# Expert weights split during the attention, routing by lists written batch by batch, and expert outputs added into x2 in memory, in one program

## What is computed

```python
x = x + tanh(g_xattn[0]) * xattn(ctx, layernorm(x), ...)   # keys and values from the context and from x itself
xf = layernorm(x)
gate_scores = softmax(xf @ gate_w)                         # 8 experts
topk_scores, topk_idx = top_k(gate_scores, 2); topk_scores /= sum(topk_scores)
h = gelu(xf @ w1[e] + b1[e]);  y = h @ w2[e] + b2[e]       # w1: 256 x 1024, w2: 1024 x 256 for each expert e
out = x + tanh(g_ffn[0]) * (topk_scores[0] * y[topk_idx[0]] + topk_scores[1] * y[topk_idx[1]])
```

## Time and profile before

| what | value |
|---|---|
| time, median of 3 runs | 1904.99 us (1902.63 to 1905.17) |
| the profiled execution's own time | 1902.62 us |
| its span in the trace | 1900.9 us |
| busy share of the span | PE 88%, PEld 61%, DVE 75%, ACT 63%, POOL 62% |
| mean granted clock of PE | 0.951 of 2.4 GHz |

### The profile page before, as it was taken

The page is one execution under the profiler, slowest core; times in us unless marked ns, Lnnn a source line. Parts: engine busy times, 40 slices in busy tenths (PEclk is TensorE's granted clock), DMA queues, the critical chain, the costliest instruction groups (busy, mean ns, idle before and its releaser), DMA issues. The chain is left out here.

```text
span 1900.9 us, 42714 instructions
## 1 busy us (share of the span) xinstructions
PE 1674.2 (88%) x15031; PEld 1163.1 (61%) x15032; DVE 1428.0 (75%) x2917; ACT 1195.3 (63%) x2666; POOL 1183.0 (62%) x1297
## 2 busy tenths in 40 slices
PE   2899999999999999999999999998402999999980
PEld 1456666666666666666666666665302999989970
DVE  4777888888888888888888888877395666666646
ACT  2587777777777777877777777777254333433320
POOL 4477777777777777777777777767263343333320
PEclk9999999999999999999999999999555999999995
DMA  3267766767767666676776776767455111111119
GB/s 131 46 127 140 142 144 131 139 139 142 147 129 145 138 140 144 135 139 138 139 150 136 136 137 129 138 130 142 118 186 173 46 49 45 50 50 47 47 35 289
DMA packets 599541, 233.18 MB, mean 123 GB/s; under 512 B 534064, under 2 KB 584016, under 8 KB 598992
## 3 DMA queue, kind: packets, MB, share of 16 engines
q1 hardware_dynamic: 592656, 212.67, 52.5%
q0 software_dynamic: 6720, 18.36, 3.1%
HBM read 78.66 MB, written 20.19 MB: 52 GB/s over the span
## 5 line engine op out<-in xcount | busy, mean ns | idle before, releaser
L279 POOL TENSOR_TENSOR p_parts<-p_f,p_parts 112x487 f16<-112x487 f32 x512 | 560.4, 1118 | 194.2 <-ACT p_parts L374 194.2
L365 ACT ACTIVATE p_f<-scores_ps,shift 112x487 f32<-112x487 f32 x512 | 337.0, 663 | 13.3 <-DVE shift L500 9.7
L495 DVE TENSOR_REDUCE neg_max<-scores_ps 112x1 f32<-112x487 f32 x512 | 313.0, 654 | 27.1 <-PE scores_ps L653 27.1
L402 ACT ACTIVATE k_hi<-proj_ps 128x488 fp32r<-128x488 f32 x256 | 147.9, 578 | 262.5 <-PE proj_ps L635 262.5
L1018 ACT ACTIVATE space<-h_ps,b_sb,undo 128x256 f32<-128x256 f32 x280 | 142.8, 560 | 232.1 <-PE h_ps L1247 228.8
L374 ACT ACTIVATE p_parts<-p_f 112x487 f16<-112x487 f32 x512 | 275.9, 607 | 0.0
L536 DVE SCALAR_TENSOR_TENSOR v_sb<-proj_ps,v_sb 128x512 f16<-128x512 f32 (+1 forms) x256 | 176.5, 689 | 92.1 <-ACT v_sb L416 89.4
L530 DVE TENSOR_TENSOR k_lo<-proj_ps,k_hi 128x488 fp32r<-128x488 f32 x256 | 168.2, 657 | 78.2 <-ACT k_hi L402 78.0
L684 PE MATMUL pv_ps<-v_sb,pt_sb 128*128 128x128 f16 x2048 | 218.9, 221 | 7.8 <-DMA pt_sb<-p_parts 7.8
L635 PE MATMUL proj_ps<-kv_hi,wkv_hi 128*128 128x488 f16 x512 | 192.3, 376 | 22.0 <-POOL kv_lo L306 13.5
L635 PE MATMUL proj_ps<-wkv_hi,kv_hi 128*128 128x512 f16 (+1 forms) x512 | 194.6, 380 | 0.1
(11 more groups left out here) (222 smaller groups left out, 4075.1 us busy)
## 6 DMA issues: line engine op xcount, KB each, us to landing
w_part<-in_L_ffn_w_dram SPq DMA_DIRECT2D x64, 256.0 KB, 3.5
stage<-in_L_ffn_w_dram SPq DMA_DIRECT2D x32, 512.0 KB, 4.1
ctx_sb<-in_ctx_dram SPq DMA_DIRECT2D x32, 375.0 KB
space<-y_rows SPq DMA_DIRECT2D x32, 224.0 KB, 4.7
pt_sb<-p_parts SPq DMA_TRANSPOSE x256, 4.0
x_sb<-in_x_dram SPq DMA_DIRECT2D x32, 112.0 KB
res_sb<-in_x_dram SPq DMA_DIRECT2D x32, 112.0 KB, 5.3
x_dram<-x_sb SPq DMA_DIRECT2D x32, 112.0 KB, 2.9
```

The lines of the kernel that those rows point to most:

```text
L279: pool.tensor_tensor(p_parts[0:LQ, p % PS, h, 1, 0:LK], p_f[0:LQ, p % 2, h, 0:LK], p_parts[0:LQ, p % PS, h, 0, 0:LK], ALU.subtract).then_i ...
L365: act.activation(p_f[0:LQ, p % 2, h, 0:LK], scores_ps[n][0:LQ, 0:LK], ACT.Exp, bias=shift[0:LQ, p // 2 % 2, n:n + 1], accum_out=row_sum[0: ...
L402: act.activation(k_hi[:, j], ps[:, 0:LKP], ACT.Copy).then_inc(kq_high, 1)
L495: dve.tensor_reduce(neg_max[0:LQ, p // 2 % 2, n:n + 1], scores_ps[n][0:LQ, 0:LK], AX.X, ALU.max, negate=True).then_inc(max_done, 1)
```

## The change

The two blocks become one. The parts are these:

- The large buffers lie in one `arena` with a 16 KB region for each expert. Peaks of w1 and w2 are taken in 32 parts in the steps of batches -1 to 14. From batch 16 on, 32 parts are loaded again, split by ACT and DVE (two operations of 128x512 each), and stored by SP to `split_dram` as float16. SP loads the finished halves into the regions: experts 0 and 1 in the last batch's steps (t = 248 to 255), 2 and 3 at t = 256, 4 to 7 after the last batch's layer norm.
- q and k are split in float16; the scale of the scores moves into the exponential. The maximum is taken over two heads in one instruction, the shift for two pairs in one.
- For each batch, DVE, PE and POOL work out the tokens' places (`onehot`, `prefix`, `rank`) and POOL writes token number and weight into `table_dram` by two indirect DMAs. The last two batches' stages stand in consecutive steps (`EARLY`). At the end one gather reads the lists, and three transposes turn them.
- ACT multiplies each tile of y by its weights, and POOL adds it by indirect DMA into `sums_dram`, which holds x2. The output is four DMAs from there, memory to memory. The expert loop is written out instead of a loop with a counter.

```diff
-        q_hi = sb("q_hi", [128, NP, LQ], F32R)
-        k_hi = sb("k_hi", [128, NP, LKP], F32R)
+        k_hi = region(4, 0, [NP, LKP], F16)
+        q_hi = region(5, 0, [NP, LQ], F16)
...
+STAGES = ("o_turn", "out", "x2", "rstd2", "xn", "xnt", "xnt_copy", "logits", "logits_copy", "top", "ratio", "onehot", "prefix", "rank", "entry")
+USUAL = dict(zip(STAGES, (13, 21, 22, 23, 24, 25, 26, 26, 27, 30, 31, 32, 34, 35, 36)))
+EARLY = {NB - 2: dict(zip(STAGES, range(13, 28))), NB - 1: dict(zip(STAGES, range(13, 28)))}
...
+            def maximum(p):
+                n = 2 * (p % 2)
+                dve.wait_ge(scores_done, 2 * p + 2)
+                dve.tensor_reduce(neg_max[0:LQ, p // 2 % 2, n:n + 2], scores_ps[0:LQ, n:n + 2, 0:LK], AX.X, ALU.max, negate=True).then_inc(max_done, 1)
...
+                if t in SPLIT_STEPS:
+                    part = SPLIT_STEPS.index(t)
+                    for w in range(2):
+                        dve.wait_ge(part_high, 2 * part + w + 1)
+                        dve.scalar_tensor_tensor(out=w_parts[:, w, 1], in0=w_part[:, w], scalar=scale[:, 4 + w:5 + w], in1=w_parts[:, w, 0],
+                                                 op0=ALU.mult, op1=ALU.subtract).then_inc(part_low, 1)
...
+                for ob in batches_at("prefix", t):
+                    pe.wait_ge(hot_done, 2 * ob + 2)
+                    nc.tensor.matmul(tail_ps(ob)[0:LQ, 264:272], before_me[0:LQ, 0:LQ], member[0:LQ, ob % 2], start=True, stop=True)
+                    nc.tensor.matmul(tail_ps(ob)[0:LQ, 272:280], ones[0:LQ, 0:LQ], member[0:LQ, ob % 2], start=True, stop=True).then_inc(prefix_done, 1)
```

The expert loop of POOL, the weighing on ACT (its loop index t handles gelu of tile t + 1), and the output:

```diff
-            for t in range(TILES + 2):
+            for t in range(TILES):
                 if t + 2 < TILES:
                     pool.wait_ge(xt_done, t + 1)
                     gather(t + 2)
-                if t >= 2:
-                    pool.wait_ge(y_ready, t - 1)
-                    for a in range(2):
-                        n = 2 * (t - 2) + a
-                        pool.indirect_dma_start(y_rows, bass.IndirectOffsetOnAxis(ap=y_row_i[:, n:n + 1], axis=0), y_sb[:, t % 2, a], None).then_inc(y_stored[t % 2], 16)
+                pool.wait_ge(y_weighed, t + 1)
+                if t >= 1:
+                    pool.wait_ge(summed[(t - 1) % 2], ((t - 1) // 2 + 1) * 32)
+                for a in range(2):
+                    n = 2 * t + a
+                    pool.indirect_dma_start(sums, bass.IndirectOffsetOnAxis(ap=sums_row[:, n:n + 1], axis=0), yw_sb[:, t % 2, a], None, compute_op=ALU.add).then_inc(summed[t % 2], 16)
...
+                    if m == 1 and t >= 1:
+                        act.wait_ge(y_ready, t)
+                        if t >= 3:
+                            act.wait_ge(summed[(t - 1) % 2], (t - 1) // 2 * 32)
+                        for a in range(2):
+                            n = 2 * (t - 1) + a
+                            last = act.activation(yw_sb[:, (t - 1) % 2, a], y_sb[:, (t - 1) % 2, a], ACT.Copy, scale=weight[:, n:n + 1])
+                        last.then_inc(y_weighed, 1)
...
+            for s in range(2):
+                sp.wait_ge(summed[s], (TILES + 1 - s) // 2 * 32)
+            per = TOKENS // 4
+            for n in range(4):
+                sp.dma_start(out.rearrange("b p d -> (b p) d")[n * per:(n + 1) * per].rearrange("(q r) d -> q (r d)", q=128),
+                             sums[n * per:(n + 1) * per].rearrange("(q r) d -> q (r d)", q=128)).then_inc(out_stored, 16)
```

1158 lines of the change are left out of this document (543 added, 615 removed).

## The result

The changed kernel takes 2486.28 us, median of 4 runs (2485.36 to 2492.66), against 1904.08 (1902.63 to 1905.17) for the kernel before on the same chip: a ratio of 1.3065, 95% interval 1.3041 to 1.309. It is slower, as forecast, but by 582 us instead of 175, and outside the range. The profiled execution's span is 2484.3 us, its mean granted clock 0.897.

The account below looks back on a forecast made before the run. PE was taken to bound the attention and the expert loop. From 1902.6 us, -28 (attention), -65 (to the first tile), -32 (end) and +300 (expert loop) made 2078, predicted as 2080; range for 8 in 10: 2010 to 2160.

Parts of the forecast that it names:

- The attention: Attention batches: float16 score blocks save PE time, gate matmuls add 16 us, DVE stays off the bound; net -28 us.
- the cover: Attention: DMA transposes of probabilities, issued two steps behind the pair, used after four, hide added weight traffic; otherwise 1 us a batch.
- Score blocks: Attention on PE: float16 matmuls save 0.35 us a block of scores, at most 45 us in all.
- The expert loop: PE waits 6.4 us a turn for a gather behind POOL's adds, clock falls: turn 20.3 us, +300 us.
- the clock's price: Expert loop: after each stall PE works at half speed for a while, costing 3.0 us a turn.
- a turn of 22.6 us: Expert loop: adds land in twice 2.46 us and the gather behind waits; time 2155 us.
- adding in memory is slow: Rival, expert loop: slow adds hold up the gather behind them; turn about 22.6 us, time 2155 us; chance 0.13.
- From the attention to the first tile: Stretch from the last attention work to the first h: first h comes earlier, -65 us, from -79 to -45.
- the 14 us charged for the loads: Before the first h: expert weight loads delay the last transpose and small routing transfers, 14 us, between 0 and 30.
- The end: From the last y to the end: 21.7 us instead of 53.9, -32 us; -19 if memory to memory runs at half rate.
- attention stretches: Rival, attention: DMA queues or DVE take the reserve, 1 us or more a batch; 2110 to 2150 us; chance 0.08.
- the likeliest case: As forecast: expert loop turn near 20 us, time 2035 to 2130 us; chance 0.60.

Follow-up runs that it names:

- port repairs: The changed kernel with the maxima of scores and the ranking's place, picked and rank kept in PSUM, order of work as changed: 2384.91 us.
- order repairs: The changed kernel with ranking, peaks and splits moved to the end of VectorE's even steps, all else as changed: 2355.77 us.
- e15_before_f16_psum: The kernel before with only the float16 parts of q and k and what goes with them, and the maxima in PSUM: 1872.76 us, ratio 0.9846.
- e3_gather_ahead: The changed kernel with the expert loop's gathers one tile further ahead in GpSimd's order, same buffers: 2163.49 us.

## Why the prediction was wrong

- **The attention, where the step failed.** The forecast said DVE goes "from 83% to some 90%" and so does not become the bound: the new work on DVE entered the sum as nothing. The added weight traffic was priced at nothing "because the DMA transpose of a pair's probabilities is issued two steps behind the pair and used after four", with 1 us a batch if the cover is gone. This is the step that failed. The busy share was no guide: DVE came out at 76% and yet a batch took 9.6 and 13.5 us more, though its blocks of scores are 1 us a batch shorter. And the cover that I looked at was that of the transposes. In the waits above PE waits for none of them, but for `q_lo`, `k_lo` and `v_lo`, two projections back, since the kernel has two banks for projections; and scores wait for the exponentials of the pairs before, since it has four score banks. Both chains run through DVE's order, and work at the end of an odd step stands in front of both.
- **What the 328 us are.** By the first scores of batch 31 (1631.4 in the changed kernel, 1303.8 before): port repairs move them by -109 (1522.6), order repairs by -128 (1503.2), both by -235 (1396.6), the maxima head by head by -59 more (1337.5). (The order repairs hold a share of the port, the splits' above.) Left are 34 us, and the 31 that float16 gives on PE: some 65 us that none of these edits undo. About 9 of them lie in batch 15, where the experts' scales are made (49.5 us there). The rest stays open.
- **The port.** "Each well under the 0.41 of L424's 256 columns", I wrote of the tiny operations, and took 2.5 us for 12. Three of them took 0.8 to 1.8 us, and four biases 0.63 each, because POOL was at work. The splits, priced at 0.69 each, took 1.54. The trace of before had a sign of it that I passed over: a bias of two columns, alone 0.16 us, took up to 0.55, and 0.40 in the mean of this group (538 to 735 us):

```profile
L500 DVE TENSOR_SCALAR shift<-neg_max 112x2 f32<-112x2 f32 x40 | 15.8, 396 | 0.7
```

  The Trainium skill says it ("SBUF — State Buffer", "Who interferes with whom"): a VectorE operation in a two-port mode, or one with two SBUF inputs beside a GpSimd operation that reads SBUF, contends with GpSimd, and the one that comes second is blocked until the first is done. The traces agree: 1.14 to 0.17, 0.81 to 0.16 and 0.63 to 0.22 us by moving one operand to PSUM.
- **Score blocks, -45 of the attention's term.** The mechanism was right, the size was 0.24 us a block instead of 0.35: 31 us, and 29 in `e15_before_f16_psum`. Without the repair at the port even this part was a loss.
- **The expert loop, +300.** Right in place, chain and size: +323.4, turn 20.76 for 20.3; the adds' issue was put too short (starts 1.31 apart, measured 2.03), the clock's price too high (3.0, measured 2.2). The time for a turn of 22.6 us comes to 2153 by the sum, not 2155. `e3_gather_ahead` takes all of it away. The rival "adding in memory is slow" fell: the gather behind the adds landed in 2.76 us, and one that stands ahead isn't delayed.
- **From the attention to the first tile, -65.** Right in sign, too large: -36.1. Without the 14 us charged for the loads the forecast was -79, and three terms were too short: the last batch's steps took 19 us more than before (60.5 for 41.4), for which the sum had nothing but those 14; the transpose between weight loads took 13.5 us for 5, the chain behind it 45 for 30. These make 43 us, -79 + 43 = -36. No run tests this stretch by itself, and what lengthens each part is not shown.
- **The end, -32.** Right: -31.5.
- **The rival "attention stretches"** named the stage and gave it 0.08 and 1 us a batch. It came together with the likeliest case, and ten times as large. "Slower" was forecast for the loop alone; that it came by 582 us is as much the attention's doing.

## What to carry to other kernels

Ask of added work not how busy its engine is but what stands behind it in the engine's order, and who waits for that; put it behind the operation that frees a buffer, not in front. Vector operations with two inputs in SBUF, however tiny, can wait there until an operation of a busy GpSimd ends, so keep one operand in PSUM. With this, the maxima head by head again, and four moves of order (ranking, peaks, splits, gathers) the changed kernel runs in 1861.64 us instead of 2486. Where a queue serves both what is wanted next and what is finished, issue the gather for a later turn before waiting for the result.
